# Graph network on one core: sorted rows loaded four per partition, z scaled four steps ahead, refills ten steps behind, one-hots a slot ahead, four banks in the second convolution

## The chip, the core and the metric

The kernel runs on one core of one Trainium2 chip. A core has five engines that run their own instruction streams side by side: TensorE (PE in the profile; its weight loads are PEld), VectorE (DVE), ScalarE (ACT), GpSimd (POOL) and SyncE (SP). They meet through semaphores. SP issues most of the DMAs, POOL the indirect ones (gathers and scatters by an index in each partition). The metric is the device time of one launch in microseconds, lower is better.

## The reference

6250 nodes with 128 features, 100000 edges `src -> dst`, sorted by `dst`; `src` is random.

```python
h = relu(layernorm(x))
# two neighbour convolutions: h1 = relu(conv(h, W1)); x = x + conv(h1, W2)
conv(h) = (segment_sum(h[src], dst) / max(deg, 1)) @ W_nbr + h @ W_root + b
h = relu(layernorm(x))
# edge-gated layer, scattered back to src
z   = concat(h[src], h[dst], edge_attr) @ W.T + b          # 256 wide
z   = batchnorm(z over all edges) * gamma + beta
msg = sigmoid(z[:, :128]) * softplus(z[:, 128:])
out = x + (h + zeros.at[src].add(msg))
```

## The kernel before

Nodes are padded to 49 windows of 128 (`NT`), edges to 196 groups of 512 (`NG`), four tiles of 128 each (`GT`). The stages follow one another:

- **Two convolutions** (`for c in range(2)`, `conv_slot`). Each does 20 iterations of 6 slots. A slot sums one gathered group: POOL gathers 4x128 rows into a ring of six (L750), DVE writes a one-hot of `dst` for each window that the group touches (L1098), PE multiplies rows by it (`sum_rows`, L1507) into bank 0 or 1, and DVE adds the finished sum of the window before to `AGG` (`add_sums`, L1090). Most groups touch one window, some two. The other edges, 19 items of 16 tiles, go through counts: DVE writes two one-hots for each tile (`hot_tile`, L1189 and L1190), PE builds a count matrix (`build`, L1493), ACT evicts it (L830), and PE multiplies the counts of the item before by the table of all nodes (`final`, L1497). The counts are built in the first convolution only; the second reads them back. Each slot also carries shares of other work: the product of a node tile with the root weights, and a step of the counting sort of edges by `src`: a one-hot of windows (`window_hot`, L1106), in the first convolution its histogram, in the second its ranks on PE (L1567, L1568) and `place_by_rank` on DVE (L1113 to L1118). 18 iterations lie in a hardware loop of two iterations, 12 slots, a round.
- The tables P and Q of the edge layer.
- **Pass 1**: z of each group, stored in `z_tab`, with its statistics.
- **Pass 2** (`in_eights`), 196 groups, rings of eight. SP loads z (L698). ACT works in fours: sigmoid (`gates`, L964), |z| (`size`, L967), exp (L973), log (L978), and between these it copies finished message rows (`take_rows`, L985, L986). DVE in its step g scales z (`scale_z`, L1389), softens group g-1 (L1396) and multiplies group g-2 (`message`, L1404). PE transposes (L1683). POOL scatters the rows of 528 B into `m_tab` in the order of `src` (L778, four a group); `take_rows` waits for the scatter of eight groups before.
- **The sorted sums.** `m_tab` is read back in 292 blocks of 512 rows (`load_sorted`, L679), each of one window: DVE writes a one-hot (L1381), PE sums (L1674), DVE adds (`add_sum`, L1374). The first 160 run inside pass 2, in its steps 120 to 183, two or three a step; the other 132 after the last scatter.

Engines take their instructions in order, and so does SP. Its step g of pass 2 is: wait until DVE scaled the group eight before, load z of g, then, for each sorted block of step g-5 (`refill`, lag 5), wait for PE's sum of it and load the block ten further on into its buffer (`MR` = 10). The first ten blocks are loaded at that place when step 120 comes up, after a wait for the scatters of the first 112 groups.

## Time and profile before

| | us |
|---|---|
| median of 3 runs | 4621.36 (4613.46 to 4630.99) |
| the profiled execution | 4617.99, its span 4616.2 |

| engine | busy us | share of the span | instructions |
|---|---|---|---|
| PE | 2990.5 | 65% | 16397 |
| PEld | 2066.4 | 45% | 16521 |
| POOL | 2530.6 | 55% | 2544 |
| DVE | 1897.1 | 41% | 4121 |
| ACT | 1408.8 | 31% | 2638 |

The page also cuts the span in 40 slices. Its row of the granted TensorE clock, in tenths of full speed, falls to 5 in pass 2:

```profile
PEclk9778777876888877889999999999555555777759
```

No engine is near 100%. The stages have different limits, so each is read by itself. In a row of the trace "[5.12 <-DVE Q L1098]" says that the engine stood idle for 5.12 us before this instruction until that line of DVE released it; "issue" means that no wait explains the gap, "remote" that the releaser isn't seen.

### The profile page before, as it was taken

To read this page: it belongs to the slowest core of one execution; us is meant where nothing else is said; L and a number is where in the kernel's file an instruction comes from. 1 tells how busy PE (TensorE), PEld (TensorE's weight loads), DVE (VectorE), ACT (ScalarE), POOL (GpSimd) and SP (SyncE) were. 2 spreads that over 40 slices of the span, in tenths; PEclk is the share of its full clock that TensorE was granted. 3 is DMA by queue.
4 is the path that set the end of the run, shared out by engine and by line. 5 is a ranking of instruction groups with operands and counts; after the bars stand their busy time and mean duration, and the time that the engine had idled before them with its cause. 6 is when DMAs were issued, how large, how long until landed. Compare 5 with 4: busy or idle time off the path is not lost.

```text
span 4616.2 us, 70620 instructions
## 1 busy us (share of the span) xinstructions
PE 2990.5 (65%) x16397; PEld 2066.4 (45%) x16521; DVE 1897.1 (41%) x4121; ACT 1408.8 (31%) x2638; POOL 2530.6 (55%) x2544
## 2 busy tenths in 40 slices
PE   1766766676878788678888888888111122555639
PEld 1444544553555555345555555555111111555529
DVE  6434434444444444632222222223332333455539
ACT  2222222212000000231211221211776777555630
POOL 4445544535565555046666666655577777555650
PEclk9778777876888877889999999999555555777759
DMA  3333333352333333157777777776544444666749
GB/s 98 121 119 115 132 126 116 105 170 84 117 113 118 116 117 118 67 185 239 230 236 236 229 234 236 228 226 203 163 138 139 138 147 143 186 195 200 221 119 274
DMA packets 449626, 749.98 MB, mean 162 GB/s; under 512 B 64824, under 2 KB 278172, under 8 KB 444384
## 3 DMA queue, kind: packets, MB, share of 16 engines
q1 hardware_dynamic: 353184, 497.82, 33.9%
q0 software_dynamic: 93440, 218.82, 16.0%
q10 hardware_dynamic: 2880, 32.11, 2.0%
q14 instruction: 95, 0.78, 0.1%
q8 instruction: 27, 0.44, 0.0%
HBM read 465.29 MB, written 283.22 MB: 162 GB/s over the span
## 4 chain that ended last, share of the span: by engine, by line
PE 42%; issue 18%; another core or an unknown queue 12%; ACT 11%; DVE 8%; DVEq 5%; DMA 2%; SPq 0%; POOL 0%; ACTq 0%; POOLq 0%
PE PS L1662 7%; PE PS L1507 6%; PE PS L1656 6%; PE PS L1647 6%; PE PS L1497 5%; PE PS L1674 5%; ACT arena L967 2%; ACT H L964 2%; PE PS L1493 1%; ACT arena L973 1%; DVEq L1096 1%; PE PS L1568 1%; DMA Q<-z_tab 1%; ACT L973 1%
## 5 line engine op out<-in xcount | busy, mean ns | idle before, releaser
L750 POOL DMA_INDIRECT Q<-h_tab,src_i x960 | 943.4, 983 | 842.1 <-PE PS L1574 403.1
L750 POOL DMA_INDIRECT arena<-p_tab,src_i x784 | 741.7, 946 | 621.8 <-issue 211.2
L778 POOL DMA_INDIRECT m_tab<-Q,pos_i x784 | 826.7, 1055 | 417.1 <-issue 231.6
L1683 PE MATMUL PS<-ident,arena 128*128 128x128 f32 x784 | 204.2, 411 | 755.5 <-issue 385.4
L1507 PE MATMUL PS<-Q 128*128 x2684 | 495.6, 341 | 191.1 <-DVE Q L1098 96.4
L1329 DVE BATCH_NORM_STATS2 stats<-arena 128x512 f32 (+1 forms) x392 | 251.5, 684 | 739.3 <-ACT arena L948 699.6
L1507 PEld LDWEIGHTS PS<-Q 128*128 128x128 f32 x2684 | 426.3, 240 | 284.5 <-issue 280.6
L948 ACT ACTIVATE arena<-PS,LB 128x512 f32<-128x512 f32 x392 | 242.6, 685 | 988.1 <-remote 825.8
L1683 PEld LDWEIGHTS PS<-ident,arena 128*128 128x128 f32 x784 | 132.6, 206 | 822.7 <-issue 712.3
L1662 PE MATMUL PS<-ident,arena 128*128 128x128 f32 x3136 | 404.4, 279 | 48.7 <-issue 47.9
L1662 PEld LDWEIGHTS PS<-ident,arena 128*128 128x128 f32 x3136 | 390.1, 195 | 86.4 <-issue 62.8
L1656 PE MATMUL PS<-arena,Q 128*128 x1341 | 341.3, 384 | 105.2 <-issue 78.0
L1647 PE MATMUL PS<-arena,WC 128*128 128x512 f32 x784 | 377.5, 602 | 18.1 <-DMA arena<-dst_tab 9.5
L1674 PE MATMUL PS<-Q 128*128 128x128 f32 x1872 | 278.6, 314 | 79.5 <-DVE Q L1381 55.2
L1098 DVE SCALAR_TENSOR_TENSOR Q<-dst_f,wneg,iota 128x512 f32 x322 | 242.7, 754 | 172.3 <-issue 172.3
L1656 PEld LDWEIGHTS PS<-arena,Q 128*128 x1464 | 143.6, 98 | 365.5 <-issue 261.7
L1674 PEld LDWEIGHTS PS<-Q 128*128 128x128 f32 x1872 | 266.4, 228 | 83.7 <-DVE Q L1381 60.6
L1493 PE MATMUL PS<-Q 128*128 128x392 bf16 x336 | 132.6, 403 | 231.1 <-DVE Q L1190 122.2
L1396 DVE SCALAR_TENSOR_TENSOR arena<-H,arena 128x512 f32<-128x512 f32 x196 | 133.8, 683 | 334.3 <-ACT arena L978 221.1
L1090 DVE TENSOR_TENSOR arena<-arena,PS x378 | 107.6, 285 | 347.6 <-PE PS L1511 162.2
L1389 DVE TENSOR_SCALAR H<-Q,bn 128x512 f32<-128x512 f32 x196 | 112.1, 572 | 243.4 <-ACT arena L967 162.9
L964 ACT ACTIVATE H<-Q,bn 128x512 f32<-128x512 f32 x196 | 146.1, 805 | 175.2 <-DMA Q<-z_tab 171.0
(221 smaller groups left out, 4174.4 us busy)
## 6 DMA issues: line engine op xcount, KB each, us to landing
z_tab<-arena SPq DMA_DIRECT2D x196, 512.0 KB
Q<-z_tab SPq DMA_DIRECT2D x196, 512.0 KB
Q<-m_tab SPq DMA_DIRECT2D x234, 264.0 KB
arena<-in_edge_t SPq DMA_DIRECT2D x196, 256.0 KB
m_tab<-arena SPq DMA_DIRECT2D x20, 2376.0 KB
m_tab<-arena SPq DMA_DIRECT2D x48, 528.0 KB
arena<-dst_tab SPq DMA_DIRECT2D x196, 128.0 KB
count_tab<-Q SPq DMA_DIRECT2D x11, 1568.0 KB
```

What stands on the lines that cost most here:

```text
L750: nc.gpsimd.indirect_dma_start(buf[:, s * GT + k, 0:width], None, table, bass.IndirectOffsetOnAxis(src_i[:, t:t + 1], 0)).then_inc(landed[ ...
L778: nc.gpsimd.indirect_dma_start(m_tab, bass.IndirectOffsetOnAxis(pos_i[:, t:t + 1], 0), mrow[:, s, k, :], None).then_inc(ms.scattered[s], 16)
L948: ins = nc.scalar.activation(zb[:, s, h * GE:(h + 1) * GE], PS[:, 2 * s + h, :], ACT.Identity, bias=LB[:, h:h + 1])
L964: nc.scalar.activation(gate[:, s, :], zin[:, s, 0:GE], ACT.Sigmoid, bias=bn[:, 10:11], scale=bn[:, 8:9])
L1098: v.scalar_tensor_tensor(onehot[:, ds(n % 2, 1), 0:n_tiles * P].rearrange("p a (t b) -> p (a t) b", b=P), bc(dst, P), wneg[:, ds(w, 1)], r ...
L1329: ins = v.bn_stats(stats[:, h, ds(g, 1), :].rearrange("p a b -> p (a b)"), zb[:, s, h * GE:h * GE + valid])
L1507: ins = mm(pair_sums(m % 2, slice(0, F)), row(t), oh[:, t * P:(t + 1) * P], start=t == 0, stop=t == n_tiles - 1, skip_group_check=True)
L1647: mm(PS[:, 2 * s + h, :], WC[:, h * F:(h + 1) * F], ebuf[:, s, :], start=True, stop=False, skip_group_check=True)
L1656: ins = mm(PS[:, 2 * s + h, :], part, hot, start=False, stop=False, skip_group_check=True)
L1662: ins = mm(PS[:, 2 * s + h, t * P:(t + 1) * P], prow[:, s * GT + t, h * F:(h + 1) * F], ident[:], start=False, stop=t == GT - 1, skip_grou ...
L1674: ins = mm(PS[:, SD + o % SD, 0:F], mrow_in[o % MR][:, t, 0:F], shot[:, o % SD, t * P:(t + 1) * P], start=t == 0, stop=t == GT - 1)
L1683: ins = turn(PS[:, 2 + q, t * P:(t + 1) * P], msg_t[:, q, t * P:(t + 1) * P], ident[:])
```

## The change

- **Layout of a sorted block.** `sorted_rows` gives partition p the rows 4p to 4p+3 of a block, one piece of 2112 B, where it gave it the rows p, 128+p, 256+p and 384+p, four pieces of 528 B.
- **Pass 2 on DVE.** `scale_z(g+4)` stands at the end of step g; it waits for the load of z, no more for `size` on ACT, and writes into eight buffers in place of four. The z load waits for `scale_z` and `size` of eight groups before.
- **Pass 2 on SP.** The refills of a step's blocks are issued ten steps later, not five. One more eight is written out ahead of the loop.
- **Convolutions on DVE.** The count one-hots and the window one-hot of slot s+1 are written in slot s (those of a round's first slot still in that slot, so that it writes two slots' share). `place_by_rank` of a slot comes after that slot's row one-hots in place of ahead of the next slot's.
- **Second convolution.** Sums rotate through banks 0 to 3 and four one-hot buffers; `AGG` gets the sum of three windows before, where it got that of one before. PE waits for `place_by_rank` of the job before it ranks the next.

```diff
+    LAG, AHEAD = 10, 4
+    CD = [2, 4]
...
+        core = [core_h[:, q, :] for q in range(SL)] + [core_s[:, q, :] for q in range(2)] + [dst_f[:, 0:GE], WAB[:]]
...
         def sorted_rows(g):
-            return m_tab[ds(g * GE, GE), :].rearrange("(t p) f -> p t f", p=P)
+            return m_tab[ds(g * GE, GE), :].rearrange("(p t) f -> p t f", p=P)
...
                     sp.wait_ge(ms.dve_step, g + 1)
+                    sp.wait_ge(ms.abs_ready, g + 1)
                     sp.dma_start(zin[:, s, :], square(z_tab, g)).then_inc(ms.z_in[s], 16)
-                at = back8(d, s, 5)
+                at = back8(d, s, LAG)
                 if at:
                     refill(*at)
...
+                at = dve.snap(before[-1], min_val=0, max_val=NT - 1)
+                a = AGG[:, ds(at, 1), cols].rearrange("p a b -> p (a b)")
+                v.tensor_tensor(a, a, pair_sums((n + 1) % k.banks, cols), ALU.add).then_inc(k.sum_added, 1)
...
                 def conv_slot(part, s, b):
                     m, u = iteration(part, s, b), s % CS
-                    for t in range(BUILT[u], BUILT[u + 1]) if part < 2 and c == 0 else ():
-                        d = m * IT + t
-                        dve.wait_ge(dn.built, d + 1)
-                        hot_tile(t, d, src_key[:, ds(d, 1)]).then_inc(dn.hot_ready, 1)
+                    slots = (CS, 2 * CS, 0)[part]
+                    for x in ([0] if s == 0 else []) + [s + 1]:
+                        if x < slots and c == 0:
+                            for t in range(BUILT[x % CS], BUILT[x % CS + 1]):
+                                d = iteration(part, x, b) * IT + t
+                                dve.wait_ge(dn.built, d + 1)
+                                hot_tile(t, d, src_key[:, ds(d, 1)]).then_inc(dn.hot_ready, 1)
...
-                    js = sort_job(part, s - 1, b)
-                    if js is not None and c == 1:
-                        place_by_rank(js)
-                    js = sort_job(part, s, b)
-                    if js is not None:
-                        if c == 0 and not (isinstance(js, int) and js == 0):
-                            dve.wait_ge(srt.hist_ready, js)
-                        window_hot(js)
+                    for x in ([0] if s == 0 else []) + [s + 1]:
+                        js = sort_job(part, x, b)
+                        if js is not None:
+                            if c == 0 and not (isinstance(js, int) and js <= 1):
+                                dve.wait_ge(srt.hist_ready, js - 1)
+                            window_hot(js, x % 2)
                     g = pool_group(part, s, b)
                     sum_by_window(k, g, words, pair, before, dst_f[:, ds(g * GT, GT)], GT)
+                    js = sort_job(part, s, b)
+                    if js is not None and c == 1:
+                        place_by_rank(js, s % 2)
...
             def scale_z(d, s):
                 g = group_of(d, s)
-                dve.wait_ge(ms.abs_ready, g + 1)
-                v.tensor_scalar(core[:, s % SL, :], zin[:, s, GE:2 * GE], bn[:, 9:10], bn[:, 11:12],
+                dve.wait_ge(ms.z_in[s], eight_of(d) * 16 + 16)
+                v.tensor_scalar(core[s], zin[:, s, GE:2 * GE], bn[:, 9:10], bn[:, 11:12],
...
-                for n, stage in ((0, scale_z), (1, soften), (2, message)):
+                if isinstance(d, int) and (d, s) == (0, 0):
+                    for n in range(AHEAD):
+                        scale_z(0, n)
+                for n, stage in ((1, soften), (2, message)):
...
+                at = back8(d, s, -AHEAD)
+                if at:
+                    scale_z(*at)
...
                         else:
                             pe.wait_ge(srt.base_in, js * 16 + 16)
-                            mm(PS[:, 6, 0:WT * NT], upper_bf[:], winhot.rearrange("p a b -> p (a b)"), start=True, stop=False)
+                            if not (isinstance(js, int) and js == 0):
+                                pe.wait_ge(srt.pos_ready, js)
+                            mm(PS[:, 6, 0:WT * NT], upper_bf[:], winhot[s % 2].rearrange("p a b -> p (a b)"), start=True, stop=False)
```

## Rows read from the trace of the kernel before

**Rows 1.** Stages: stretch, length, each engine's busy us (instructions), clock, DMA share, GB/s.

```profile
70.00:1003.00 933.00, 642.24 (x4487) 455.74 (x4488) 387.72 (x1164) 216.37 (x614) 456.04 (x465) 0.79 0.35 120
1107.00:1885.00 778.00, 617.90 (x3020) 406.31 (x3020) 353.66 (x779) 40.23 (x162) 421.28 (x432) 0.81 0.37 117
...
3240.00:3915.00 675.00, 131.18 (x472) 84.48 (x472) 206.36 (x357) 492.79 (x804) 481.93 (x460) 0.50 0.48 146
3920.00:4365.00 445.00, 258.45 (x1444) 239.78 (x1443) 232.13 (x479) 248.20 (x408) 260.18 (x244) 0.74 0.66 196
4365.00:4478.00 113.00, 32.17 (x149) 25.58 (x148) 35.20 (x67) 60.12 (x103) 80.86 (x78) 0.55 0.33 111
4478.00:4600.00 122.00, 120.91 (x1056) 120.72 (x1056) 116.99 (x266) 0.00 (x0) 0.00 (x0) 0.97 1.17 289
```

**Rows 2.** Groups by line, 3300 to 3915: busy, mean ns, idle before, releasers.

```profile
L778 POOL DMA_INDIRECT m_tab<-Q,pos_i x430 | 451.2, 1049 | 164.4 <-issue 129.7 <-ACT Q L986 34.7
L985 ACT COPY Q<-PS 128x512 f32<-128x512 f32 x107 | 61.4, 574 | 171.3 <-remote 95.8 <-issue 61.9 <-PE PS L1683 13.6
```

**Rows 3.** The same groups by line, 3920 to 4365.

```profile
L778 POOL DMA_INDIRECT m_tab<-Q,pos_i x244 | 260.8, 1069 | 185.1 <-ACT Q L986 115.6 <-issue 69.5
...
L964 ACT ACTIVATE H<-Q,bn 128x512 f32<-128x512 f32 x60 | 46.2, 808 | 170.4 <-DMA Q<-z_tab 166.6 <-issue 3.6
```

**Rows 4.** SP's own waits, 3920 to 4365: line, releaser, us, times, longest.

```profile
SPq L679 <- PE PS L1674: 135.8, 69, 8.7
```

**Rows 5.** Timeline around 4090: start, us, engine, line, instruction, idle before.

```profile
4086.16 6.87 SPq L679 DMA_DIRECT2D Q<-m_tab  x2
...
4093.19 0.29 DVE L1374 TENSOR_TENSOR arena<-arena,PS 128x128 f32 x1 [5.66 <-PE PS L1674]
...
4093.92 0.34 SPq L698 DMA_DIRECT2D Q<-z_tab  x1
...
4098.33 0.81 ACT L964 ACTIVATE H<-Q,bn 128x512 f32<-128x512 f32 x1 [11.89 <-DMA Q<-z_tab]
...
4099.99 0.97 POOL L778 DMA_INDIRECT m_tab<-Q,pos_i  x1 [7.64 <-ACT Q L986]
```

**Rows 6.** Groups by line, 4480 to 4598, the sums after the last scatter.

```profile
L1381 DVE TENSOR_TENSOR Q<-Q,iota 128x512 f32<-128x512 f32 x104 | 71.4, 686 | 1.4 <-issue 1.4
```

**Rows 7.** First convolution, 120 to 980: PE's largest wait (us, times, longest).

```profile
PE PS L1493 <- DVE Q L1190: 120.1, 42, 12.4
```

**Rows 8.** First convolution, timeline: a round's first slot, and later ones.

```profile
241.07 0.51 PE L1493 MATMUL PS<-Q 128*128 128x392 bf16 x1 [8.61 <-DVE Q L1190]
...
511.20 0.25 DVE L1189 TENSOR_SCALAR Q<-Q 128x128 bf16<-128x128 int16 x1 [6.96 <-issue]
...
527.66 0.34 PE L1493 MATMUL PS<-Q 128*128 128x392 bf16 x1 [2.11 <-DVE Q L1190]
...
887.11 0.51 PE L1493 MATMUL PS<-Q 128*128 128x392 bf16 x1 [12.38 <-DVE Q L1190]
```

**Rows 9.** Second convolution, 1150 to 1860: PE's waits, and POOL's gathers by line.

```profile
PE PS L1507 <- DVE Q L1098: 51.0, 21, 7.2
PE PS L1567 <- DVE Q L1106: 35.2, 24, 4.3
PE PS L1507 <- DVE arena L1090: 14.8, 21, 4.5
...
L750 POOL DMA_INDIRECT Q<-h_tab,src_i x417 | 406.3, 974 | 289.3 <-issue 113.2 <-PE PS L1574 97.5 <-remote 78.6
```

**Rows 10.** Second convolution, timeline around 1260.

```profile
1253.93 1.16 PE L1507 MATMUL PS<-Q 128*128 x8
...
1257.90 0.92 PE L1568 MATMUL PS<-Q,ones 1*128 1x392 f32 x2
...
1262.80 0.57 DVE L1113 TENSOR_TENSOR Q<-PS,Q 128x392 f32<-128x392 f32 x1 [5.01 <-remote]
...
1266.53 3.75 PE L1507 MATMUL PS<-Q 128*128 x16 [5.12 <-DVE Q L1098]
```

## What the change should do to the time

> **What bounds the kernel now.** The first view is the table of stages [rows 1]: no engine fills a stage except the last one, where PE is busy for 120.91 and DVE for 116.99 of 122 us. So each stage is read for the wait that ends last in it. The views of groups by line and of waits come second, and the timeline third, to see the order inside one wait.
>
> Pass 2 has two halves. From 3300 to 3915, ahead of the sorted sums, POOL issues 430 scatters: 451.2 us busy, 129.7 us of "issue" gaps between them, and only 34.7 us of waiting for rows from ACT [rows 2]. Four scatters make a group, so POOL needs 4 x (451.2 + 129.7) / 430 = 5.40 us a group, and the half runs at 4 x (451.2 + 164.4) / 430 = 5.73. It is bound by POOL, with ACT's row copies next: they wait 95.8 us for a releaser that isn't seen, which by the code is the scatter of eight groups before, since PE's transposes had ended. From 3920 to 4365, beside the sorted sums, POOL needs the same, 4 x (260.8 + 69.5) / 244 = 5.41, yet runs at 4 x (260.8 + 185.1) / 244 = 7.31, because it waits 115.6 us for ACT; and ACT waits 166.6 us for the load of z, over 60 groups, so 15 fours, 11.1 us each [rows 3]. Why the load is late stands in SP's queue: SP waits 135.8 us for PE at its refills [rows 4]. The timeline shows one turn: SP stands at a refill from 4086.16 to 4093.03, released as DVE gets PE's sum at 4093.19; only then it issues z, at 4093.92; ACT starts at 4098.33 after 11.89 us idle, POOL at 4099.99 after 7.64 [rows 5]. The reader is to see a ring: z waits for a refill, the refill for a sum of step g-5, the sum for DVE's step, that step for ACT, and ACT for z.
>
> In the convolutions PE is busy for 69% (642.24 of 933) and 79% (617.90 of 778) at a granted clock of 0.79 and 0.81 [rows 1], and its gaps are waits for DVE. First convolution: 120.1 us, 42 times, for the count one-hots [rows 7]. Eight of the 42 are long, one a round, 8.61 the first and 12.38 us the last [rows 8]; read one by one in the timeline they make 73.3. There DVE itself stands for 6.96 us of "issue" at the top of a round. The other 34 make 46.8, 1.4 us each, as at 527.66 [rows 8]. Second convolution: 51.0 us for row one-hots, 35.2 for the window one-hot, 14.8 for adds, 101 in 66 waits [rows 9]. Around 1260 one sees how: ranks end on PE at 1258.82, DVE's `place_by_rank` gets them at 1262.80, its row one-hot comes behind that in the queue, and PE idles 5.12 us [rows 10].
>
> **Pass 2, refills ten steps behind and z scaled ahead.** At lag 10 SP waits for a sum five steps older, some 5 x 7.3 = 36 us, against the 11.1 us that ACT waits for z each time. I take all of that wait off. DVE's scaling no longer waits for ACT, so the sums of a step that followed it come earlier too. The refill keeps up: the block of step h is needed at step h+4, and SP issues it once ACT has taken |z| of group h+2, before the logarithms on which step h+4 hangs. What is late next is POOL, and behind it the ring of eight rows. Floor 5.41 us a group, as it needs now; the half without sums runs at 5.73 with 146 GB/s; beside the sums the traffic would rise from 196 to 196 x 7.31 / 5.9 = 243 GB/s [rows 1], so scatters land later than there. I take 5.9, near the 5.73: 61 groups x (7.31 - 5.9) = 86 us gained. Bounds: 117 us at the floor, 25 us at 6.9, if scatters landing late take back most.
>
> In the half without sums the same edits can remove at most POOL's 34.7 us; they don't touch the scatter ring, so I take 5. The piece from 4365 on is POOL's backlog (80.86 us busy in 113, [rows 1]) and stays. The first ten blocks are asked for at SP's step 130, not 125: DVE may start its sums up to 10 us late once, with eight groups of rows to cover POOL. Nothing is taken, 10 in the range. The scaling's new wait for z, ahead of the next step on DVE, is a load issued since SP passed the refills of step g-7; nothing, too, and the rival below is what it costs uncovered. The move of `scale_z` adds no instruction.
>
> **The layout.** After the last scatter 104 of DVE's one-hots have 1.4 us of idle time ahead of them in all [rows 6], none of it for a DMA, and DVE and PE are busy for 116.99 and 120.91 of 122 us [rows 1]: they set the 0.92 us a block (120.91 for 1056 matmuls, eight a block). Nothing, 0 to 4 us for the first loads. In the sorted half it eases a DMA share of 0.66 [rows 1]; it is in the 5.9. The Trainium skill, page "DMA: Bandwidth & Descriptors", section "How a descriptor splits into AXI transactions", says that a piece that doesn't start on a 256 B boundary fetches from the boundary below. A row of 528 B mostly starts off one, so by an estimate from that page four pieces cost an eighth to a sixth more beats than one of 2112 B. No run here shows it yet, and at 289 GB/s in a stage that DVE fills it would change nothing.
>
> **First convolution.** The 34 short waits go, as DVE has a slot's lead; its one-hots of rows come after the same number of instructions as before. The eight long ones stay: the round's first slot is still written in itself, with three more tiles and a window one-hot (about 2 us) ahead of the row one-hot, covered by PE's three builds, finals, root and histogram, some 5 us. If that cover fails it costs 8 to 9 x 2 = 18. I take 40 of 46.8, and 5 for the clock: after such a gap PE runs at half clock, where 16 matmuls take 3.75 us against 1.16 for 8 at full clock [rows 10], 1.6 times as long. Gain 45, bounds 0 and 80. The wait for `hist_ready` is for the same histogram as before.
>
> **Second convolution.** One-hots now stand ahead of `place_by_rank`, and adds wait for sums three windows back, so DVE can be late by the 4 to 5 us of the example without PE noticing. In slots 10 and 11 there is no sort step, so DVE also gets ahead before the round's stop. Two thirds of the 101 us: 67. The clock: 0.81 means that 38% of the stage is at half clock (1.2 GHz, the rest 2.4). If fewer gaps bring that to 30%, PE's 618 us shrink by 618 x 0.08 x 0.6 / 1.23 = 24. Gain 91, bounds 20 and 140. It can't pass POOL: 4 x (406.3 + 113.2) / 417 = 4.98 us a slot, 598 us for 120 slots of the 778. PE's new wait for the placing of the job before is met some 4 us ahead. Two register moves more a window lie in DVE's idle half.
>
> Row and page disagree on the four banks. The rows show gaps from DVE's order, with two banks. The Trainium skill, page "TensorE: Matmul & The Clock Gate", section "A second HAM failure mode: psum-queue depth-cycling", tells of a kernel that lost clock by rotating through PSUM banks with small idles between groups. Here the adds would wait less, so I give it a small chance, below.
>
> **The sum.** 86 + 5 + 45 + 91 = 227 us. The profiled execution took 4617.99 us (span 4616.2), 3 us under the median of 4621. 4618 - 227 = 4391, and by the median 4394. I predict 4393.
>
> **The rivals.** (1) The scatter ring takes over: ACT's 95.8 us of waits [rows 2] stand for scatters that land some 30 us after issue, and more traffic makes that later. Pass 2 gives 25 instead of 91: 4459. For it: these waits exist already at 146 GB/s. Against: POOL still needs 5.40 of the 5.73 us there, so the ring cost a third of a microsecond a group. (2) PE isn't really idle in the convolutions: its releases are seen late, ranks 4 us after their end [rows 10], so the gaps shown may be paid elsewhere. The convolutions give 30 instead of 136: 4499. Both together: 4565. (3) All terms near their upper bounds, pass 2 130, convolutions 80 and 130: 4278. (4) Slower: `scale_z` of g+4 finds z not landed and holds DVE with the soften, message and sums of step g+1 behind it, PE's transposes and POOL's scatters behind those. Place: steps 120 to 183. Price: 11.1 us each four steps on DVE on top of today's, 15 x 11.1 = 166. It decides once z lands later than four steps after SP's issue, over 20 us, where rows 5 show 4.1 us (4094.26 to 4098.33). With half of the convolutions' 136: 4618 + 166 - 68 = 4716. (5) The rotation through four banks breaks PE's stream: the second convolution falls to pass 2's clock of 0.50 [rows 1]. Its 618 us are 618 / 1.23 = 502 at full clock and 804 at half: 186 lost, with 91 + 45 gained elsewhere 4668; it eats those 136 from 84% of the time at half clock on, a clock of 0.58. The skill's page above is its rule. (6) The edits find other covers and nothing moves: 4610.
>
> **How the numbers follow.** Forecast 0.46 (own range 4340 to 4450), (1) 0.17, (2) 0.16, both 0.05, (3) 0.08, (4) 0.03, (5) 0.02, (6) 0.03. A range of 4290 to 4565 leaves out (4) to (6) and most of (3), 0.14. A measurement of this kernel tells 0.5%, 23 us, from no change: faster is 0.92, same 0.03, slower 0.05.
>
> **What would show it.** Right: ACT's wait for z in the sorted half under 30 us, SP's wait at refills no longer ahead of z, POOL at 5.9 us a group, pass 2 shorter by some 90 us. In the first convolution the short waits for one-hots gone and eight or nine long ones left; in the second under 40 us of PE waiting for DVE and a clock of 0.84 or more. The last stage at 122 us. Wrong: POOL waiting for ACT and ACT for "remote" (1); gaps of DVE at z (4); convolutions that keep 930 and 780 us with fewer waits shown (2).

## The result, and the profile after

The changed kernel takes 4513.07 us (median of 4 runs, 4506.80 to 4524.36) against 4620.17 for the kernel before, a ratio of 0.9769 with a 95% interval of 0.9749 to 0.9790: 107 us (2.3%) faster, inside the range, and under half of the 227 us that the forecast took off. The profiled execution took 4524.36 us (span 4522.6), 11 over its median, so its trace has 94 us to show, not 107. The stages first, from the table of stages of the changed kernel; columns as in rows 1.

```profile
64.00:982.00 918.00, 623.74 (x4482) 442.79 (x4482) 388.44 (x1168) 221.06 (x621) 460.66 (x470) 0.81 0.36 122
1077.00:1850.00 773.00, 609.33 (x3013) 398.14 (x3014) 350.52 (x781) 40.85 (x164) 426.63 (x434) 0.81 0.37 118
3207.00:3890.00 683.00, 130.63 (x471) 84.27 (x472) 204.61 (x362) 493.16 (x805) 479.18 (x459) 0.50 0.45 144
3900.00:4300.00 400.00, 252.49 (x1536) 230.71 (x1536) 244.92 (x510) 264.15 (x431) 282.84 (x259) 0.77 0.71 235
4385.00:4506.00 121.00, 120.19 (x1056) 120.06 (x1056) 115.92 (x266) 0.00 (x0) 0.00 (x0) 0.98 0.90 291
```

The last stage is what it was. The sorted half of pass 2 carries most of the gain: its clock and its traffic rose (0.74 to 0.77, 196 to 235 GB/s). The convolutions won 19 us and 15 by the starts of the node products in the timeline. Their PE time, busy and idle, was summed over each whole convolution (first: from the launch to the first node product; second: from the last node product of the first to the first of the second). Set side by side are the first pair of profiles, the second pair (`e_before_again` and `e_after_again`, group C below) and one more run:

```
                conv 1: us   PE busy   idle     conv 2: us   PE busy   idle   clock 1, 2
before              1001.0     642.0   359.0         866.9     658.6   208.3   0.80, 0.79
after                982.1     623.8   358.3         851.6     650.4   201.2   0.82, 0.79
e_before_again       996.6     632.7   363.9         864.4     653.5   210.9   0.82, 0.79
e_after_again        977.4     630.0   347.4         845.4     650.6   194.8   0.81, 0.79
e_two_banks          964.6     621.3   343.4         866.7     655.8   210.9   0.85, 0.79
```

In the first pair nearly all of the first convolution's gain stands in PE's busy time (18 us for the same matmuls) and 1 us in its gaps; in the second pair 3 us and 16. So a gain of this size can't be split into clock and gaps from one pair. In the second convolution the gaps gave 7 us in one pair and 16 in the other.

Stage lengths, read from the timeline in every run: up to the first node product, from the last of those to the first of the second node stage, on to the first scatter, then to the first scatter of group 115, from there to the last scatter, and the rest.

```
kernel          group of runs   conv 1   conv 2  to pass 2  g 0-115  g 115-195   rest
before          first pair      1001.0    866.9     1375.8    655.9      556.9  143.5
after           first pair       982.1    851.6     1380.8    662.2      487.0  142.7
e_conv          A                964.2    829.1     1356.9    654.5      515.7  143.9
e_pass2         A                987.8    854.7     1359.0    655.9      481.8  142.2
e_lag5          A                958.7    844.5     1357.6    655.2      525.8  142.0
e_rows_apart    A                966.8    841.2     1358.2    653.8      484.4  143.6
e_after         B                836.9    705.5     1165.7    625.2      450.0  142.3
e_half_finals   B                836.1    689.9     1164.6    627.2      450.6  142.2
e_narrow_finals B                837.3    684.6     1167.3    626.0      449.2  142.2
e_long_rounds   B                773.9    729.1     1167.2    626.5      447.1  142.1
e_before_again  C                996.6    864.4     1376.3    657.0      558.4  143.8
e_after_again   C                977.4    845.4     1381.2    662.0      491.2  142.9
e_two_banks     C                964.6    866.7     1378.1    661.3      484.9  142.0
e_long_first    C                938.8    848.7     1379.7    662.5      487.9  142.9
e_after_third   D                975.9    844.5     1378.4    664.0      490.9  142.8
e_half_finals_2 D                971.4    831.6     1376.6    661.6      489.1  143.0
e_ring6         D                983.8    852.9     1384.6    663.8      489.1  142.6
e_best          D                932.3    851.3     1377.9    662.2      489.8  142.6
e_ranks_alone   E                973.4    829.7     1383.1    662.9      493.0  142.0
e_flat_first    E                906.4    854.9     1383.1    664.2      487.9  141.6
```

Groups A to E are runs taken together on one chip. The kernel before took 4531, 3957, 4624, 4623 and 4629 us in them, so kernels are compared inside a group where it can be done. A stage whose code is the same still moves from profile to profile: the first convolution of `e_two_banks`, `e_ring6` and `e_after_third` takes 965, 984 and 976 us, the second of `e_conv`, `e_lag5` and `e_rows_apart` 829, 845 and 841. So a difference under some 20 us is read only where it comes again in several profiles.

Pass 2 beside the sums, groups by line of the changed kernel from 3900 to 4300:

```profile
L786 POOL DMA_INDIRECT m_tab<-Q,pos_i x259 | 283.7, 1096 | 117.5 <-issue 74.2 <-ACT Q L997 43.2
...
L975 ACT ACTIVATE H<-Q,bn 128x512 f32<-128x512 f32 x64 | 46.9, 804 | 0.2
...
L996 ACT COPY Q<-PS 128x512 f32<-128x512 f32 x64 | 37.1, 579 | 134.4 <-remote 92.6 <-PE PS L1720 33.6 <-issue 8.1
```

SP's own waits at the refills, in the kernel before from 3920 to 4365 (beside the 135.8 us of [rows 4]), then in the changed kernel from 3900 to 4300:

```profile
SPq L679 <- remote: 104.0, 15, 21.5
```

```profile
SPq L686 <- PE PS L1711: 113.2, 51, 7.1
SPq L686 <- remote: 52.8, 18, 5.3
```

ACT's gate (L975 here), which waited 166.6 us for z [rows 3], has no wait for z left in this stretch. SP still waits at its refills, 166.0 us where it waited 239.8, but for sums of ten steps back, so that the z load behind them is out in time. POOL runs at 4 x (283.7 + 117.5) / 259 = 6.20 us a group, where it ran at 7.31; it needs 4 x (283.7 + 74.2) / 259 = 5.53, as a scatter takes 1096 ns at 235 GB/s where it took 1069 at 196.

The convolutions, PE's waits in the changed kernel: first convolution from 120 to 961, then the second from 1120 to 1826 (us, times, longest).

```profile
PE PS L1539 <- issue: 63.4, 42, 5.5
PE PS L1525 <- DVE Q L1208: 55.9, 13, 8.3
PE PS L1539 <- DVE arena L1103: 45.8, 29, 5.6
PE PS L1539 <- DVE Q L1113: 28.4, 21, 4.5
PE PS L1525 <- ACT arena L841: 19.5, 17, 2.1
```

```profile
PE PS L1539 <- DVE Q L1113: 34.9, 24, 5.0
PE PS L1539 <- issue: 28.0, 34, 3.6
PE PS L1583 <- ACT Q L879: 26.1, 8, 5.7
PE PS L1539 <- DVE arena L1103: 14.9, 17, 3.2
PE PS L1601 <- DVEq L1135: 9.4, 6, 4.0
```

The count one-hots' waits [rows 7] fell from 120.1 us in 42 to 55.9 in 13; eight long ones, 53.9 of it by the timeline, are left, so the short ones are gone but for 2 us. Yet `issue` and the adds' waits at L1539 rose by 61 (63.4 and 45.8; in the kernel before, 120 to 980, 30.9 and 17.2 at L1507). In the second the 101 us of waits for DVE [rows 9] became 59 (34.9, 14.9, 9.4), and ACT's and `issue` took their place. In the second pair such waits fell from 81 to 68 us only.

The eight long waits of the first convolution are still there, but 19.4 us shorter in sum (73.3 to 53.9). DVE's own idle time ahead of its two count one-hots may say why, in the kernel before (200 to 920) and in the changed one (200 to 900):

```profile
L1190 DVE TENSOR_SCALAR Q<-Q 128x392 bf16<-128x392 int16 x249 | 81.9, 329 | 24.7 <-issue 24.4
L1189 DVE TENSOR_SCALAR Q<-Q 128x128 bf16<-128x128 int16 x248 | 67.2, 271 | 59.0 <-issue 59.0
```

```profile
L1208 DVE TENSOR_SCALAR Q<-Q 128x392 bf16<-128x392 int16 x249 | 82.8, 332 | 0.6
L1207 DVE TENSOR_SCALAR Q<-Q 128x128 bf16<-128x128 int16 x249 | 65.1, 261 | 67.8 <-issue 62.0 <-PE PS L1525 5.7
```

In the kernel before DVE stood still a second time in each round, ahead of L1190, for 1.8 to 5.6 us. The 83.4 us of `issue` became 62.0, and in the second pair 80.6 became 65.9. That is about what the stage won, and it comes with the new order of DVE's instructions. That it is the cause is argued; no run separates it.

### The profile page after: what moved, and what is told of

It reads as the page before. It is cut to its first block, busy times and chain, and to the rows that moved or that the text cites. A ratio compares the mean times of both kernels' runs of the same rounds, so it can differ in the third digit from the quotient of the medians.

```text
span 4522.6 us, 70374 instructions
## 1 busy us (share of the span) xinstructions
PE 2938.9 (65%) x16397; PEld 2024.3 (45%) x16521; DVE 1883.7 (42%) x4125; ACT 1409.7 (31%) x2638; POOL 2541.3 (56%) x2544
## 4 chain that ended last, share of the span: by engine, by line
PE 39%; issue 19%; another core or an unknown queue 17%; ACT 11%; DVE 8%; DVEq 5%; DMA 1%; ACTq 0%; POOL 0%; SPq 0%; POOLq 0%
PE PS L1699 6%; PE PS L1539 6%; PE PS L1693 5%; PE PS L1529 5%; PE PS L1684 5%; PE PS L1711 4%; ACT H L975 2%; PE PS L1525 1%; PE PS L1602 1%; ACT arena L978 1%; ACT arena L984 1%; DVEq L1111 1%; DVEq L398 1%; ACT L984 1%
## 5 line engine op out<-in xcount | busy, mean ns | idle before, releaser
L1539 PE MATMUL PS<-Q 128*128 x2684 | 483.6, 333 | 263.8 <-issue 111.6
L1539 PEld LDWEIGHTS PS<-Q 128*128 128x128 f32 x2684 | 412.5, 233 | 360.7 <-issue 357.6
L1711 PE MATMUL PS<-Q 128*128 128x128 f32 x1872 | 262.2, 303 | 64.2 <-issue 55.7
L1711 PEld LDWEIGHTS PS<-Q 128*128 128x128 f32 x1872 | 251.5, 218 | 71.3 <-issue 59.6
L996 ACT COPY Q<-PS 128x512 f32<-128x512 f32 x196 | 112.7, 575 | 342.1 <-remote 232.1
L1684 PEld LDWEIGHTS PS<-arena,WC 128*128 128x128 f32 x784 | 135.8, 193 | 124.6 <-issue 123.8
L1404 DVE TENSOR_TENSOR Q<-Q,iota 128x512 f32<-128x512 f32 x234 | 160.2, 685 | 47.5 <-DMA Q<-m_tab 34.5
```

What stands on the lines that cost most here:

```text
L1539: ins = mm(pair_sums(m % k.banks, slice(0, F)), row(t), oh[:, t * P:(t + 1) * P], start=t == 0, stop=t == n_tiles - 1, skip_group_check=True)
L1684: mm(PS[:, 2 * s + h, :], WC[:, h * F:(h + 1) * F], ebuf[:, s, :], start=True, stop=False, skip_group_check=True)
L1711: ins = mm(PS[:, SD + o % SD, 0:F], mrow_in[o % MR][:, t, 0:F], shot[:, o % SD, t * P:(t + 1) * P], start=t == 0, stop=t == GT - 1)
```

## The experiments

**Group A: which part gives what.** `e_pass2` is the kernel before with the edits of pass 2:

```diff
+        core = [core_h[:, q, :] for q in range(SL)] + [core_s[:, q, :] for q in range(2)] + [dst_f[:, 0:GE], WAB[:]]
...
-                at = back8(d, s, 5)
+                at = back8(d, s, 10)
...
+                at = back8(d, s, -4)
+                if at:
+                    scale_z(*at)
```

> The kernel before with the three edits of the second pass alone (rows of m in one piece, z scaled four steps ahead, refills ten behind); both convolutions as before. The changed kernel's trace puts 64 us of its gain between the first and the last scatter of this pass. Theory A (the parts are independent): 55 to 75 us under the kernel before, near 4553. Rival B (part of that came from the convolutions, since the changed clock and the earlier start shift the pass): 25 to 45 us under it. The forecast had 91 here.

Measured: 4492.52 us against 4531.48, ratio 0.9913 (0.9889 to 0.9937), 39 us: rival B's number. Its reason is tested by the next run. `e_conv` is the changed kernel with exactly those edits undone.

> The changed kernel with the three edits of the second pass undone: only the convolutions' edits are left (one-hots a slot ahead, two window one-hots, four banks in the second). Theory A (independent parts): the 34 us that the changed trace shows by the end of the second convolution, so 25 to 45 us under the kernel before, near 4587. Rival B: 60 us or more, when the second pass's 64 us were partly theirs. The forecast had 136 here.

Measured: 4499.66 us, ratio 0.9936 (0.9913 to 0.9958), 32 us. Theory A: the convolutions alone give what the first pair's trace showed, so pass 2's gain wasn't partly theirs. Pass 2 gives less than its 64: by the table its part from group 115 on is 34 us shorter (515.7 to 481.8), where the first pair won 70. What shrank is the cost of the old order, 515.7 us here against 556.9 there; the new one takes 481.8 against 487.0. A wait that is taken off gives what it cost in the runs at hand.

```diff
-    LAG, AHEAD = 10, 4
+    LAG, AHEAD = 5, 4
```

> The changed kernel with its refills five steps behind again, z still scaled four steps ahead and one piece per partition. If the queue order was what made z late (a refill on SP waits for TensorE's sums of five steps ago and the next z load stands behind it), z scaled four ahead now needs its load even sooner and the stall moves to VectorE: 30 us or more slower than the changed kernel, over 4540. If scaling ahead was enough by itself: within 10 us of it, 4503 to 4523.

Measured: 4516.46 us, 15 under the kernel before (0.9974, 0.9957 to 0.9991), though the convolutions' 32 are in it: with refills five behind, scaling ahead gives pass 2 nothing (525.8 against 515.7). The bounds written down were set for the first chip. The changed kernel itself wasn't run in this group; by the two parts it would take 4531 - 71 = 4460, so a lag of five costs about 56, and 47 against the next run, which differs by the lag and the layout. The groups by line of `e_lag5`, 3865 to 4165, show the old wait alive:

```profile
L975 ACT ACTIVATE H<-Q,bn 128x512 f32<-128x512 f32 x44 | 33.8, 808 | 88.1 <-DMA Q<-z_tab 87.7 <-issue 0.2
```

and the same line in `e_rows_apart`, 3870 to 4170, where refills are ten behind:

```profile
L975 ACT ACTIVATE H<-Q,bn 128x512 f32<-128x512 f32 x48 | 35.2, 804 | 0.2
```

So scaling ahead gives nothing without the lag of ten. My expectation put the stall on DVE; it stayed on ACT, which needs the same z. The lag of ten without the scaling ahead wasn't run, so whether the lag would do it alone isn't known.

```diff
-            return m_tab[ds(g * GE, GE), :].rearrange("(p t) f -> p t f", p=P)
+            return m_tab[ds(g * GE, GE), :].rearrange("(t p) f -> p t f", p=P)
```

> The changed kernel with the sorted messages' rows read as before (four rows of 512 bytes per partition, 128 rows apart) instead of one piece. The forecast put this edit at nothing: within 5 us of the changed kernel, 4508 to 4518. Rival: the 112,000 packets that the one piece saves clear the queues in which the scatters also stand, then the sorted groups go slower by 0.3 us or more each, 61 of them, 20 us or more: over 4533.

Measured: 4469.39 us, 62 under the kernel before, where the parts measured apart make 71. From group 115 on it takes 484.4 us, `e_pass2` with the one piece 481.8, and the last stage 143.6 against 142.2. So the layout is worth 0 to 4 us by the stages and up to 9 by the medians, too little to tell from nothing here, though it removes 112,000 of 450,000 packets. The rival's 20 us didn't come. (A row has 528 bytes, not the 512 of the expectation.)

**Group B: the changed kernel elsewhere, TensorE's load, the rounds' length.**

> The changed kernel itself on this chip, so that the other runs have it beside them. Its gain should be the sum of the parts measured apart (39 us for the second pass, 32 us for the convolutions, and what the one piece per partition adds to them, 0 to 10): 65 to 80 us under the kernel before, if the chip behaves as the one of those runs; 107 under it if it behaves as the first one.

Measured: 3944.03 us against 3957.25, ratio 0.9967 (0.9956 to 0.9978): 13 us, which is neither of the two. In this trace no wait has the releaser `remote` at all, which in the first pair's trace of after names 2383 us over all engines. DVE's wait for the ranks, groups by line from 1000 to 1500, and POOL's gathers to 1520:

```profile
L1128 DVE TENSOR_TENSOR Q<-PS,Q 128x392 f32<-128x392 f32 x77 | 43.5, 564 | 77.3 <-PE PS L1602 76.9
...
L758 POOL DMA_INDIRECT Q<-h_tab,src_i x383 | 382.7, 999 | 138.1 <-issue 108.1 <-PE PS L1608 30.0
```

Here POOL gathers at 4 x (382.7 + 138.1) / 383 = 5.44 us a slot, of which 5.13 are its own; in the changed kernel of the first pair 4 x (410.9 + 288.6) / 418 = 6.69. On this chip the second convolution lies close above POOL's gathers. The kernel before was timed here but not profiled, so which stage's gain is missing wasn't seen. What makes releases late on the others isn't known; packets and instructions are the same in number.

`e_half_finals` makes only the final products of even windows, `e_narrow_finals` all but the first and the last at 128 columns (its edit isn't shown):

```diff
+                            if c == 0 or w % 2 == 0:
+                                ins = final(par, w)
```

> The changed kernel with only every second of the final products of the second convolution (it leaves out half of that sum; its instructions and its array time go together). Those products are 864 matmuls with 188 us of recorded busy time in the second convolution. Theory A (TensorE's own stream is what the second convolution waits for, so that emptier gaps elsewhere change nothing): 70 to 95 us under the changed kernel. Theory B (the forecast's: its waits for VectorE, and their latency, are the bound, so more room on TensorE gives little): less than 25 us under it.

> The changed kernel with the final products of the second convolution at 128 of their 384 columns in all but the first and last window (it leaves out two of the three parts of the sum; the number of instructions stays 864 in that stage, and only array time goes). If theory A holds and it is array time that binds: each goes from 366 ns towards the 180 ns of a one-column product there, some 150 us less busy, 70 us or more under the changed kernel. If it holds and it is the instructions' supply that binds: within 15 us of the changed kernel though the halved one gains. Under theory B both stay within 25 us.

Measured: 3924.33 and 3924.15 us, 20 under the changed kernel both, with 16 and 21 of it in the second convolution. By the numbers written down that is theory B, but the clock spoils the test, as the table of stages of `e_after`, then `e_half_finals`, then `e_narrow_finals`, 1000 to 1500, shows:

```profile
1000.00:1500.00 500.00, 429.76 (x2391) 284.93 (x2392) 282.03 (x629) 32.11 (x132) 367.07 (x368) 0.90 0.44 143
```

```profile
1000.00:1500.00 500.00, 414.81 (x2110) 279.89 (x2108) 291.83 (x654) 33.55 (x136) 371.40 (x381) 0.84 0.46 149
```

```profile
1000.00:1500.00 500.00, 414.28 (x2465) 305.49 (x2463) 290.61 (x649) 32.74 (x133) 370.42 (x380) 0.79 0.46 150
```

With less to do PE was granted less clock, 0.90, then 0.84 and 0.79, and the matmuls left took longer: those of the row sums 309 ns on the mean in `e_after` and 333 with half of the final products gone. PE's busy time in the second convolution fell from 581.2 to 551.0 us, by 30 where 94 were taken away; most came back as slower work. The narrow products keep every instruction and gain no less, so it isn't the supply of instructions that binds.

`e_long_rounds` has both convolutions' loops in 3 rounds of 36 slots:

```diff
-            with eng.Fori(0, PAIRS) as b:
-                for s in range(2 * CS):
-                    slot(1, s, b)
+            with eng.Fori(0, PAIRS // 3) as q:
+                for j in range(3):
+                    for s in range(2 * CS):
+                        slot(1, s, q * 3 + j)
```

> The changed kernel with each convolution's loop written as 3 rounds of 36 slots in place of 9 rounds of 12; the same work in the same order. In the first convolution TensorE starts 32 matmuls in the 18 us about a jump back, on the mean of eight, where its mean rate would give 91: 11.6 us lost per jump, 93 us in that stage; in the second nothing of the kind shows. Theory A (the loss belongs to the jump back, as the engines must fetch the round's start anew): six jumps fewer in each convolution, 40 to 70 us under the changed kernel, all before the first node product. Theory B (the loss belongs to the work at the round's top, one-hots and counts that start late): within 10 us of the changed kernel. Theory C (code in a straight line is fetched no faster than after a jump): slower by 10 us or more.

Measured: 3905.36 us, 39 under the changed kernel: theory A's 63 us in the first convolution, and 24 lost in the second. Why the first gains shows at a round's top in the changed kernel's timeline; DVE jumps back at 322.4:

```profile
322.11 0.29 DVE L1103 TENSOR_TENSOR arena<-arena,PS  x1 [7.18 <-remote]
...
328.98 0.25 DVE L1207 TENSOR_SCALAR Q<-Q 128x128 bf16<-128x128 int16 x1 [6.58 <-issue]
...
329.52 0.51 PE L1525 MATMUL PS<-Q 128*128 128x392 bf16 x1 [8.34 <-DVE Q L1208]
```

DVE waits for no semaphore in those 6.58 us. What moves is the queue that loads instructions: in the DMA view of the changed kernel it has these lines from 321 to 334, in the whole loop of the first convolution (234 to 953), and in that of the second (1171 to 1813).

```profile
q14 instruction: 3, 0.02, 0.5%
```

```profile
q14 instruction: 44, 0.36, 0.2%
```

```profile
q14 instruction: 3, 0.02, 0.0%
```

The columns are packets, MB and share. By these counts the first convolution's loop is fetched anew in each round, the second's is not; with 36 slots a round the second's too (27 and 29 packets on two queues). Whether the 24 us went there isn't shown: in `e_long_rounds` DVE's `issue` waits in the second convolution are 3 us longer at the row one-hots (137.2 against 134.2), PE's idle time is the same (125.8 against 124.3), and its busy time rose from 581.2 to 603.3 us, at a clock of 0.83 in place of 0.87.

**Group C: one chip for both kernels, the banks, long rounds where they pay.**

> The kernel before, profiled on the chip of this group, since the gain was 107 us on the first chip and 13 us on the third, where the kernel before itself took 3957 us in place of 4620. The stages' ends of both kernels on one chip tell which stage's gain it is that goes with the chip. Theory A (on a chip where no engine's sequencer is held up for 0.7 us at a time, gathers on POOL bind the second convolution, at 1.25 us each, and the refills never made z late): the changed kernel is within 5 us in the second convolution and within 15 us in the second pass there. Theory B: all stages' gains shrink alike.

Measured: 4623.69 us. This group's chip took 4620 and not 3957 us, so the theories weren't tested; the run served as the second pair.

> The changed kernel on the chip of this group, as the run that the others of the group are compared with. By the three chips so far: 13 us under the kernel before where that takes about 3957 us, 70 to 107 under it where it takes 4530 to 4620.

Measured: 4518.63 us, ratio 0.9767 (0.9741 to 0.9794), 105 us: the first pair again, stage by stage in the table (conv 1 19, conv 2 19, groups from 115 on 67).

```diff
-    CD = [2, 4]
+    CD = [2, 2]
```

> The changed kernel with two banks and two one-hots in the second convolution, as in the first and as before; the rest stays changed. Theory A (the second convolution is bound by POOL's gathers, or by releases that come late, and not by TensorE's waits for the next one-hot): within 8 us of the changed kernel. Theory B (the forecast's: the four banks give most of the second convolution's 91 us): 40 us or more slower than the changed kernel. Rival C (more banks spread the stream and cost): 5 us or more faster.

Measured: 4533.78 us, 15 slower than the changed kernel, with 21 more in the second convolution (866.7 against 845.4): between A and B. The total is noisy (four runs from 4515 to 4544), but the stage is clear when all profiles on chips like this one are read: with two banks 864, 867 and 867, with four 845 to 855. Four banks and their four row one-hots, which the run takes back together, are all of what the second convolution won; with two it stands at the kernel before's 864.4, though window one-hots are made ahead.

`e_long_first` has long rounds in the first convolution alone (`per = 3 if c == 0 else 1`).

> The changed kernel with 3 rounds of 36 slots in the first convolution and the second's 9 rounds of 12 left alone. VectorE stands still for 6.7 and again 5.6 us behind its jump back in the first convolution, with the loads of the instruction queue landing at the end of each, and not in the second. Rounds of 36 in both took 63 us off the first convolution and put 24 on the second. Theory A: 50 to 70 us under the changed kernel, since the first keeps its gain and the second its time. Theory B (the later stages take it back): less than 40.

Measured: 4484.60 us, 34 under the changed kernel. The second convolution kept its time, so A's mechanism, at B's size: the first gave 39, where the faster chip gave 63.

**Group D: the second convolution again, and the scatter ring.**

> The changed kernel as the run beside which the others of this group are read: 4510 to 4525 us if the kernel before takes 4620, about 3944 if that takes 3957.

Measured: 4517.45 us against 4623.41.

> The changed kernel with every second final product of the second convolution left out (half of that sum is missing), once more, since on the chip that takes 3957 us it gave 20 of TensorE's 94 us of busy time and the second convolution there stood 0.07 us a gather above POOL's floor of 1.25 us. Theory A (on the slower chips, with 0.42 us a gather of slack, TensorE's stream is the bound): 60 us or more under the changed kernel. Theory B (a circle of waits between TensorE, VectorE and ScalarE, each seen late): 15 to 45. Theory C (TensorE has nothing to do with it): under 10.

Measured: 4509.66 us, 8 under the changed kernel (C's number), 13 in the stage, with the clock down from 0.82 to 0.73 in the stage (1130 to 1790), and the ranks' second matmul (L1602) took 681 ns in place of 607. Again no clean test.

```diff
+                if not (isinstance(d, int) and d == 0 and s < 6):
+                    act.wait_ge(ms.scattered[(s + 2) % RZ], (eight_of(d) + (1 if s >= 6 else 0)) * (16 * GT))
```

> The changed kernel with the second pass's rows of m in a ring of six: ScalarE also waits for the scatters of the group six back, in place of eight. Rival 1 of the forecast (the ring of landings takes over and gives the groups their rate): 8/6 of 6.0 us a group in the groups with sorted sums, 80 of them, up to 160 us slower; over 20 slower if it binds now and then. If the ring does not bind (a scatter lands 4.5 us behind its issue by the trace on the faster chip): within 8 us of the changed kernel.

Measured: 4532.51 us, 15 over the changed kernel, but not in pass 2: 489.1 us from group 115 on against 490.9, and 663.8 against 664.0 ahead of it. The ring doesn't bind. The 15 us stand in stages whose code is the same, and are within what such stages move. ACT's waits at the row copy, 3930 to 4230 here, are as long as with a ring of eight (100.0 us against 101.5 in `e_after_third`), a full ring ahead of a busy POOL, which costs nothing:

```profile
L998 ACT COPY Q<-PS 128x512 f32<-128x512 f32 x49 | 28.3, 577 | 100.0 <-remote 90.0 <-PE PS L1722 7.2 <-issue 2.7
```

`e_best` has the long first rounds, and the ranks placed a slot later, in banks 6 and 7 by turns:

```diff
+                    if c == 1:
+                        js = sort_job(part, s - 1, b)
+                        if js is not None:
...
+                            place_by_rank(js, (s - 1) % 2)
+                        hots_of_windows([s + 1])
```

> The changed kernel with two more edits: the first convolution in rounds of 36 slots (34 us under the changed kernel in the run before this), and in the second convolution the ranks placed a slot later, behind the next slot's one-hots, in two banks by turns. VectorE idles about 190 us of the second convolution ahead of the ranks' first operation. Theory A (that wait holds back the one-hots and with them the stage): 50 to 70 us under the changed kernel in all, 20 to 35 of it in the second convolution. Theory B (one-hots are already ahead of TensorE, four deep, and the wait costs nothing): 30 to 42 us in all. Theory C (TensorE now waits for the bank instead): under 30.

Measured: 4469.74 us, 48 under the changed kernel; the first convolution gave 44 and the second took 7 more (851.3 against 844.5). The total falls between A's range and B's, but A's 20 to 35 in the second convolution didn't come: placing the ranks later gains nothing there.

**Group E: the wait for the ranks gone, and no jump back.** In `e_ranks_alone` DVE works on the window one-hot itself. It waits for the ranks only later, before it writes over their one-hot, and PE no longer waits for the placing:

```diff
-                dve.wait_ge(srt.ranked, i + 1)
+                dve.wait_ge(srt.winhot_ready, i + (1 + JOBS))
...
-                v.tensor_tensor(ranked, PS[:, 6, 0:WT * NT], winhot[par].rearrange("p a b -> p (a b)"), ALU.mult
+                v.tensor_tensor(ranked, winhot[par].rearrange("p a b -> p (a b)"), winhot[par].rearrange("p a b -> p (a b)"), ALU.mult
```

> The changed kernel in which VectorE no longer waits for the ranks in the second convolution: TensorE makes them as before, but nobody reads them (four window one-hots by turns; VectorE does the same three operations on a window one-hot, and the rows are scattered in the order of their numbers, so that the sorted sums are of the wrong rows). Only the second convolution's time is read. Theory A (the circle of late releases runs through this wait, some 190 us of VectorE's time): 40 us or more less than the changed kernel's 845 to 852 us there. Theory B (it runs elsewhere, through the one-hots and the root's copies): less than 15. Theory C: between the two, each circle has its share, as POOL's own 600 us of gathers and the slow start lie beneath.

Measured: 829.7 us in the second convolution, 15 to 16 under the changed kernel's in C and D: at B's edge. The changed kernel wasn't run in this group, and the same code moved by as much between profiles, so the gain is at most small. The 195 us of DVE's waits for the ranks in the changed kernel (130.4 `remote` and 64.2 PE) are gone, and in their place the waits view (1120 to 1800) has

```profile
DVE Q L1256 <- ACT Q L848: 108.6, 14, 13.8
```

DVE now waits for ACT, which takes the final products' row. The wait removed uncovers another.

`e_flat_first` writes out the first convolution's nine rounds.

> The changed kernel with all 108 slots of the first convolution's loop written out, no jump back in it. Rounds of 36 slots, six jumps fewer of eight, took 37 us off the first convolution, 6 us a jump. Theory A (it is by the jump): two more, 45 to 55 us under the changed kernel, near 4468. Theory B (code read in a row has a cost too, which the saved jumps had paid so far): 20 to 40 under it.

Measured: 4461.06 us, ratio to the kernel before 0.9640 (0.9606 to 0.9674), the fastest of all; some 57 under the changed kernel's 4518 of C and D, theory A. (The kernel before takes 4629 us in this group and 4624 and 4623 in those.) DVE's count one-hots, groups by line from 200 to 900, in the changed kernel and then here:

```profile
L1207 DVE TENSOR_SCALAR Q<-Q 128x128 bf16<-128x128 int16 x249 | 65.1, 261 | 67.8 <-issue 62.0 <-PE PS L1525 5.7
```

```profile
L1212 DVE TENSOR_SCALAR Q<-Q 128x128 bf16<-128x128 int16 x260 | 66.1, 254 | 1.5 <-remote 1.3
```

The 62.0 us of `issue` are gone, and the first convolution is 70 us shorter than in the changed kernel of C and D. Code in a straight line is fetched too (24 and 33 packets on the two queues), and DVE doesn't stand still for it at these one-hots. Its second convolution is 10 us longer and takes 40 packets where the changed kernel's takes 3, though its code is the same; why wasn't asked.

## Why the prediction was right, and where it was wrong

The range of 4290 to 4565 held the time and the sign was right, but the likeliest case, 4393, was 120 us off. The range held a convolution gain that came out at a quarter of the forecast because it was wide; that part of the hit is luck. Of the rivals, (2) fits best: the convolutions give 34 us by the trace, where it said 30 and the forecast 136, and its 4499 is 14 us from the median. Its reason, gaps that are paid elsewhere, fits the experiments; that late releases are what pays them isn't shown.

**Second convolution, 91 forecast, 15 measured (19 in the second pair).** This is the failed step. "Two thirds of the 101 us: 67" took the sum of PE's waits for DVE as time of the stage. The waits did shrink, by 42 us, and PE's idle time over the whole convolution by 7 (208.3 to 201.2); in the second pair by 13 and 16. `e_two_banks` says that window one-hots ahead give nothing and four banks with their one-hots 15 to 21; `e_best`, `e_ranks_alone` and the two with fewer products say that no single wait or load there is worth over 21. Several circles may run side by side: one-hots and sums, ranks and their placing, the root's turn and copy, final products and their row. That together they bind was argued, as no run removed two; why the stage stays as long as it is is open. The 24 us for the clock had no ground of their own: it was to rise to 0.85 with fewer gaps, and it stayed (0.81 and 0.81).

**First convolution, 45 forecast, 19 measured (19 in the second pair).** The short waits went as foretold (46.8 to 2), and eight long ones stayed. But `issue` and add waits took the place of the short ones, so "40 of 46.8" is the second term that failed by the same mistake: PE's idle time in the whole convolution fell by 1 us in one pair and by 16 in the other. What the stage won is near what DVE stood still less at the round's top, 21 and 15 us, which the forecast didn't have. The larger sum stood where it passed by: "There DVE itself stands for 6.96 us of issue" was read in the profile and not asked after. It goes with the jump back and the fetch of the round's code, and `e_flat_first` shows 70 us in it.

**Pass 2 beside the sums, 86 forecast, 70 measured from group 115 on (67 in the second pair).** The mechanism is right: no wait for z on ACT, POOL at 6.20 us a group. The size is off where 5.9 was chosen: POOL's own need rose from 5.41 to 5.53 with the traffic, and 43.2 us of waits for ACT are left, 0.67 a group. 61 groups at 6.20 in place of 5.9 are 18 us, against the 16 that lack. `e_lag5` shows that the refills' place was part of the cause, as the ring of [rows 4, 5] says. (The bound "117 us at the floor" is 61 x (7.31 - 5.41) = 116.)

**Pass 2 ahead of the sums, 5 forecast, minus 6 measured (minus 5).** POOL's waits for ACT didn't shrink: 37.9 us from 3270 to 3890, where they were 34.7 from 3300 to 3915. The stretch is 5 to 6 us longer in both pairs; why is open. Inside the stated 0 to 34.7 it was not.

**Layout 0, last stage 0.** Measured 0 to 4 in group A. The Trainium skill's page "DMA: Bandwidth & Descriptors", section "How a descriptor splits into AXI transactions", let one expect an eighth to a sixth more beats for four pieces. Worked out again from its table, as an estimate, it is 82 beats on the mean against 69, a fifth more. The packets fell by a quarter and no stage took notice.

**The rivals.** (1) is out: with a ring of six pass 2 keeps its time. The rows that spoke for it, 95.8 us of ACT's waits, were a full ring, that is a POOL which sets the pace; and where (1) has scatters land some 30 us after issue, `e_after`, the one trace that shows it, has 4.5 on the median. (3) is out. (4) didn't occur: DVE's scaling waited 6.9 us for z in the whole run. (5) didn't occur either: the clock of the second convolution is 0.81 as before, and two banks are slower than four. What the Trainium skill's page "TensorE: Matmul & The Clock Gate" tells in the section "A second HAM failure mode: psum-queue depth-cycling" of another kernel didn't happen in this one. (6) is out.

The sum as it came out: 70 - 6 + 0 + 19 + 15, and minus 5 ahead of pass 2, whose cause is open, make 93 of the 94 us; the other 13 of the medians' 107 are the profiled runs' own places, after's 11 over its median and before's 2 under.

## What to carry to other kernels

A sum of named waits on one engine is not yet a gain. In the two convolutions the waits that the edits aimed at fell by 42 and 64 us, and the stages by 15 and 19, since others took their place. Take such a term at what the other loops of handoffs leave, and judge it by the engine's idle time over the whole stage, in more than one pair of profiles: a single pair put 1 us into the gaps of a stage where the next put 16. Where a wait reads `issue` at the top of a long written-out loop, look at the instruction queue; here a loop whose code was fetched each round paid at each jump back, and fewer rounds or none saved 39 and 70 us, while the same edit made another loop 24 us longer. Refills behind which another engine's loads queue belong so many steps back that what they wait for is long past.

## What the runs showed of the hardware

The jump back. In the first convolution instructions were loaded anew in each round (44 packets of 8 KB in the loop), and DVE stood still for 6.58 us behind the jump; on the chip of group B for 6.9 to 7.3 and, after two tiles, 2.9 to 5.4 more. The second convolution's loop needed 3 packets in all and showed no such stop in each round (DVE's long `issue` waits there are five ahead of L1128, 15.0 us in all); written three times as long it needed 56. The Trainium skill, page "Runtime: NRT & Kernel Launch", section "Instruction fetch mechanics", has each engine's instruction RAM refilled in blocks of 16 KiB, and an engine stopped behind a taken branch whose target isn't loaded, until it is fetched. The trace agrees on the stop and shows how long it is; it has such blocks on one queue (28, 0.46 MB in the whole run) and blocks of half that on the other (97, 0.79 MB).

The chips. The same two kernels differ by 107, about 71 (the two parts of group A), 13 and 105 us. On the chip of group B the changed kernel needs 3944 us in place of 4519, with the same packets and matmuls; its trace names no late release, where those of the first pair and of groups C and D have 2383 to 2465 us of them and `e_conv` of group A 1758. The cause is open. The chips of groups A and C carry the same number, 11, though the kernel before took 4531 and 4624 us in them, so it may not be the chip alone. From 13 to 107 us: for this change, which removes waits, it mattered more where and when it ran than which of its parts were in.

TensorE's clock. With half of 864 products gone in a stage the granted clock fell from 0.82 to 0.73, and from 0.90 to 0.84 on the faster chip; the stage won 13 and 16 us. PE was busy for 77% and 82% of that stage, and work taken off it came back in large part as clock.
